# SyncE fetches one column of node rows in every second round of a four-layer graph network

## What is computed

```
x = layernorm(x + L0(x, src, dst))       # q,k,v: softmax over the edges of a node of q[src].k[dst]; sums v[src]
x = layernorm(x + L1(x, edge_attr_64))   # (x[src] + bond) @ W, softmax over the edges, sum, batch norm
x = layernorm(x + L2(x, edge_attr_64, _n2, _n3))  # message and key from [x[src], eh], query from [qrh, qeh]
x = layernorm(x + L3(x, edge_attr_32))   # relu([x[src], ea] @ w1 + b1) @ w2, mean over the edges, update
```

## Time and profile before

| | us |
|---|---|
| median of 3 runs | 9012.55 |
| the profiled execution | 9008.73 |
| its span, first to last instruction | 9006.9 |
| POOL busy | 6622.4 |
| DVE busy | 4898.5 |
| ACT busy | 3185.7 |
| PE busy | 2211.0 |

### The profile page before, as it was taken

The page is one execution under the profiler, slowest core; times in us unless marked ns, Lnnn a source line. Parts: engine busy times, 40 slices in busy tenths (PEclk is TensorE's granted clock), DMA queues, the critical chain, the costliest instruction groups (busy, mean ns, idle before and its releaser), DMA issues. The chain is left out here.

```text
span 9006.9 us, 54907 instructions
## 1 busy us (share of the span) xinstructions
PE 2211.0 (25%) x11915; PEld 1737.2 (19%) x11915; DVE 4898.5 (54%) x6124; ACT 3185.7 (35%) x3856; POOL 6622.4 (74%) x6997
## 2 busy tenths in 40 slices
PE   3000000000200000000046666666654222222224
PEld 1000000000200000000026666666643010101013
DVE  5356565655747777777744454444545333333335
ACT  0123222222513222232324555455544333333332
POOL 6777777777677777777757777777765777777776
PEclk6555555555555555555558888888877565656556
DMA  9233333333123333333323343434322333333332
GB/s 359 81 111 105 110 109 109 109 110 113 35 78 102 114 102 114 102 109 106 100 84 121 130 137 129 138 125 138 130 86 76 124 114 122 116 122 116 116 122 83
DMA packets 367104, 1037.46 MB, mean 115 GB/s; under 512 B 164320, under 2 KB 172410, under 8 KB 352272
## 3 DMA queue, kind: packets, MB, share of 16 engines
q1 hardware_dynamic: 136048, 670.35, 19.8%
q0 software_dynamic: 224608, 342.26, 14.7%
q10 hardware_dynamic: 6336, 23.79, 0.7%
HBM read 634.02 MB, written 401.90 MB: 115 GB/s over the span
## 5 line engine op out<-in xcount | busy, mean ns | idle before, releaser
L787 POOL DMA_INDIRECT g<-x_table,edge_ix x1512 | 1427.8, 944 | 460.8 <-issue 460.8
L787 POOL DMA_INDIRECT se<-x_table,edge_ix x1512 | 1426.8, 944 | 460.8 <-issue 460.8
L787 POOL DMA_INDIRECT hidden<-hidden_table,edge_ix x1512 | 1426.6, 944 | 460.8 <-issue 460.8
L787 POOL DMA_INDIRECT qv<-qv_table,edge_ix x1484 | 1400.2, 944 | 452.3 <-issue 452.3
L925 ACT ACTIVATE edge_sums<-edge_val 128x1904 f32<-128x1904 f32 (+3 forms) x220 | 1115.2, 5069 | 459.8 <-DVEq L1616 459.8
L915 DVE TENSOR_TENSOR_SCAN edge_val<-edge_bank,edge_val 128x464 f32<-128x464 f32 (+1 forms) x715 | 687.6, 1032 | 360.4 <-ACT edge_val L1578 354.0
L1570 PE MATMUL edge_e_ps<-w_nodes,edge_ea_t 128*128 128x512 f32 x784 | 474.8, 771 | 1466.9 <-DVEq L1610 1458.4
L868 ACT ACTIVATE edge_bank<-edge_weight_arg 128x112 f32<-128x112 f32 (+3 forms) x169 | 38.6, 228 | 2131.2 <-DVE edge_decay_arg L859 2131.2
L1609 DVE TENSOR_TENSOR hidden<-hidden,edge_e_ps 128x3584 f32<-128x3584 f32 x55 | 213.8, 3888 | 842.3 <-DMA hidden<-hidden_table,edge_ix 791.8
L1476 DVE TENSOR_TENSOR edge_product<-mk_ps,edge_q_now 128x256 f32<-128x256 f32 x392 | 166.6, 425 | 898.5 <-ACT edge_msg L1415 897.5
L1578 ACT ACTIVATE edge_val<-hidden 128x3584 f32<-128x3584 f32 x55 | 348.8, 6342 | 785.6 <-DVEq L1610 785.6
(11 more groups left out here) (425 smaller groups left out, 8468.6 us busy)
## 6 DMA issues: line engine op xcount, KB each, us to landing
sums<-edge_sums SPq DMA_DIRECT2D x56, 1848.0 KB, 7.0
sums<-edge_sums SPq DMA_DIRECT2D x55, 1792.0 KB, 6.2
sums<-edge_sums SPq DMA_DIRECT2D x56, 1008.0 KB, 4.0
sums<-edge_sums SPq DMA_DIRECT2D x55, 924.0 KB, 3.8
edge_k<-k_edges SPq DMA_DIRECT2D x56, 896.0 KB, 4.6
edge_bond<-in_edge_attr SPq DMA_DIRECT2D x56, 896.0 KB, 8.3
edge_eh<-in_edge_attr SPq DMA_DIRECT2D x56, 896.0 KB
edge_qr<-in_edge_attr_n SPq DMA_DIRECT2D x56, 896.0 KB
```

The costliest lines, as they stand in the source:

```text
L787: e.indirect_dma_start(self.gather_into(u, j), None, self.gather_from, bass.IndirectOffsetOnAxis(ap=now[:, j:j + 1], axis=0))\
```

## The change

In rounds 4, 6, ... 26 of layer 0, and 2, 4, ... 26 of the other layers, POOL leaves out the last column (27) of the chunk b = 1. SP fetches these 128 rows itself. It reads the 128 node numbers of the column, at most 22 at a time, from a new input `src_aside` in memory into registers, and issues for each number one transfer of one row, its address from the register, into one partition of a new tile `aside`. It does this in three portions (43, 43, 42 rows) in its turns for three chunks: both of the round before, and the first of the round itself. Behind the third portion it waits for all 128 rows and issues one transfer that copies `aside` into column 27 of the gather buffer (`place`). Then the hardware loop of SP has two rounds in its body. The last column of chunks b = 1 gets semaphores of its own, `last_in` when POOL gathers it and `placed` when SP does, and whoever waits for the last part waits for these as well.

```diff
@@ -32,6 +32,8 @@
 QUAD = 4
 ENDS, LATE = (4, 3), 3
 FD = 64
+BATCH = 22
+ASIDE = (slice(0, 43), slice(43, 86), slice(86, P))
 HEADS = 8
 FAR = -1.0e30
 SKIPPED = 1.0e9
@@ -79,6 +81,8 @@
         assert self.chunks % 2 == 0 and self.groups % 2 == 0 and J % QUAD == 0
 
         self.find_rows, self.find_cols = ins["dst_table"].shape
+
+        self.gather_width = (2 * FD, FD, FD, P)
 
         def dram(name, shape, dt=F32):
             return nc.dram_tensor(name, shape, dt).ap()
@@ -684,6 +688,10 @@
         self.part_summed, self.tail_ready = self.sem("part_summed"), self.sem("tail_ready")
         self.cut = 0
         self.passed = self.sem("passed")
+        self.steady = self.alone + 1
+        self.aside = self.sb("aside", [P, p.gather_width[layer]])
+        self.aside_in, self.placed = self.sem("aside_in"), self.sem("placed")
+        self.last_in = self.sem("last_in")
         self.bank = self.ps("bank", [P, 512])
         self.taken_of_bank = 0
         if h:
@@ -731,20 +739,54 @@
             e.sem_inc(self.stored[b], 1)
             load(b, b)
 
-        def turn(i):
+        def turn(i, beside=lambda b: None):
             for b in (0, 1):
                 for c in range(self.parts):
-                    self.wait_part(e, i, b, c)
+                    self.wait_part(e, i, b, c, placed=False)
                 load_index(b, bass.ds(i * (2 * J) + (2 + b) * J, J))
                 hold(e, self.attr_free[b], at(i, 1, 1), self.passed)
                 load(b, i * 2 + (2 + b))
+                beside(b)
                 hold(e, self.ready[b], at(i, 1, 1), self.passed)
                 store(b, rows_of(i, b, J))
 
-        for i in range(self.alone):
+        def fetch(k, rows):
+
+            for first in range(rows.start, rows.stop, BATCH):
+                now = slice(first, min(first + BATCH, rows.stop))
+                _, numbers = p.nc.values_load_multi_w_load_instructions(
+                    p.ins["src_aside"][bass.ds(k + (self.steady + 1) // 2, 1), now],
+                    engines=[mybir.EngineType.SP], min_val=0, max_val=p.n_rows - 1,
+                    skip_runtime_bounds_check_because="src holds node numbers below n_nodes")
+                for r, number in zip(range(now.start, now.stop), numbers):
+                    e.dma_start(self.aside[r:r + 1, :], self.gather_from[bass.ds(number, 1), :])\
+                        .then_inc(self.aside_in, 16)
+
+        def place(i, k):
+
+            hold(e, self.aside_in, at(k, 16 * P, 16 * P), self.passed)
+            hold(e, self.rows_free[1], at(i, 1, 1), self.passed)
+            u = self.buffer(i, 1)[0]
+            e.dma_start(self.gather_into(u, J - 1), self.aside[:, :]).then_inc(self.placed, 16)
+
+        e.sem_inc(self.placed, 1)
+        for i in range(self.steady):
             turn(i)
-        with e.Fori(self.alone, self.rounds - 1) as i:
-            turn(i)
+        with e.Fori(0, (self.rounds - 1 - self.steady) // 2) as k:
+            one = k * 2 + self.steady
+
+            def beside_one(b):
+                if b == 0:
+                    hold(e, self.placed, at(k, 16, 1), self.passed)
+                fetch(k, ASIDE[b])
+
+            def beside_two(b):
+                if b == 0:
+                    fetch(k, ASIDE[2])
+                    place(one + 1, k)
+
+            turn(one, beside_one)
+            turn(one + 1, beside_two)
         for b in (0, 1):
             if b and self.cut:
                 self.store_cut(e)
@@ -782,11 +824,27 @@
                     else:
                         e.wait_ge(self.rows_free[b], i + 1)
                 for j in range(J):
-                    if J * n + j < done:
+                    if J * n + j < done or (b and j == J - 1 and i in self.with_aside):
                         continue
                     e.indirect_dma_start(self.gather_into(u, j), None, self.gather_from,
                                          bass.IndirectOffsetOnAxis(ap=now[:, j:j + 1], axis=0))\
-                        .then_inc(self.gathered[u][j * self.parts // J], 16)
+                        .then_inc(self.last_in if b and j == J - 1 else self.gathered[u][j * self.parts // J], 16)
+
+    @property
+    def with_aside(self):
+        return range(self.steady + 1, self.rounds - 1, 2)
+
+    def wait_last(self, e, i, placed):
+
+        if isinstance(i, int) and i <= self.steady:
+            e.wait_ge(self.last_in, 16 * (i + 1))
+            return
+        alone = ((i + (2 + self.steady)) >> 1) * 16
+        if not placed:
+            hold(e, self.last_in, alone, self.passed)
+        else:
+            e.wait_ge(self.last_in, alone)
+            e.wait_ge(self.placed, at((i - (self.steady - 1)) >> 1, 16, 1))
 
     def buffer(self, i, b):
 
@@ -796,10 +854,25 @@
             return ((0, (0, 0, 1)), (1, (0, 0, 1)), (2, (0, 0, 1)), (0, (0, 0, 2)))[2 * i + b]
         return 1 - b, (i, 1, b)
 
-    def wait_part(self, e, i, b, c):
+    def wait_part(self, e, i, b, c, placed=True):
         u, (times, per, more) = self.buffer(i, b)
         columns = 16 * J // self.parts
-        e.wait_ge(self.gathered[u][c], at(times, per * columns, more * columns))
+        if c < self.parts - 1:
+            e.wait_ge(self.gathered[u][c], at(times, per * columns, more * columns))
+            return
+        if not self.begun:
+            e.wait_ge(self.gathered[u][c], at(i, columns - 16 * b, columns - 16 * b))
+        elif isinstance(i, int) and i < 2:
+            e.wait_ge(self.gathered[u][c], (columns, columns - 16, columns, 2 * columns - 16)[2 * i + b])
+        else:
+            more = columns if b else -16
+            if placed:
+                e.wait_ge(self.gathered[u][c], at(i, columns - 16 * b, more))
+            else:
+                hold(e, self.gathered[u][c - 1], at(i, columns, columns * b), self.passed)
+                hold(e, self.gathered[u][c], at(i, columns - 16 * b, more), self.passed)
+        if b:
+            self.wait_last(e, i, placed)
 
     def wait_gathered(self, e, i, b):
         for c in range(self.parts):
@@ -2552,6 +2625,8 @@
             full = a.reshape(1) if a.ndim == 0 else a
         arrays[name] = full
     arrays["src"] = arrays["src"].view(np.uint32)
+    ends = arrays["src"].reshape(P, edges_pp // (2 * J), 2 * J)[:, 0::2, 2 * J - 1]
+    arrays["src_aside"] = np.ascontiguousarray(ends.transpose(1, 0))
     return arrays
 
 
```

## The result

The changed kernel takes 9808.67 us (median of four runs, 9807.54 to 9812.9) where the kernel before takes 9011.03. The ratio is 1.0886, with a 95% interval of 1.0867 to 1.0905. The forecast was 8949.

What follows compares the result with a forecast made beforehand. POOL's unbroken row of gathers was taken as the bound: 51 fewer at 1.2485 us give 63.7 us, with SP's fetch and the waits free, so 9012.55 became 8949 us; own range 8943 to 8956, stated range 8940 to 8995.

Steps and rivals of the forecast that it cites:

- The forecast gain of 63.7 us: Edge phases on POOL: 51 gathers fewer, each taking away its whole pace of 1.2485 us.
- The cost on the path is nothing: SP's 128 row transfers and register loads per two rounds fit beside POOL's work and add no time.
- one trip a read: SP's reads of node numbers: six memory trips of 1.4 us per 128 rows, 0.07 us a row, plus 0.06 a number.
- c: Price on SP of one fetched row, number read included: taken as 0.62 us, with ends at 0.48 and 2.2.
- Late columns are free until POOL itself finds the buffer occupied: Placed column in layer 1: up to 15.8 us of lateness costs nothing, as VectorE frees the buffer before POOL returns.
- at about 0.9 us a row: Row price on SP where the change was to turn from gain into loss; lateness passes 15.8 us at 0.87.
- that formula: Lateness of the placed column in a pair of rounds, 128c - 95.7 us, once a row costs over 0.77 us.
- only the store and the next index list: What stands on SP behind the wait for all 128 rows; POOL wants the list a chunk later, so cost nothing.
- Rival A: SP's number reads: one memory trip per number, 1.96 us a row, SP becomes the bound, 15,300 us; chance 0.12.
- B: SP's small transfers disturb POOL's own issue in the fetching chunks: 89 us more than now, 9102 us; chance 0.04.
- C: Layer 1's saturated stretch delays SP's first rows, or row price near 0.88: part of gain lost, 8960 to 8995; chance 0.04.
- D: SP's row price sits on the crossing and the gain is just gone: 8995 to 9030 us; chance 0.03.

Runs made afterwards that it cites:

- the other order alone: Changed kernel, reads still unaligned, with SP's sums stored one turn later and its row fetch put ahead of the attribute-tile wait and load: 8984.4 us, ratio 0.9969.

## Why the prediction was wrong

**Right: what bounds the kernel and what a gather is worth.** The forecast gain of 63.7 us is what the kernel with aligned reads and an early fetch has: 9011.66 - 8947.81 = 63.9. The tail of the phases kept its length in that kernel, though not in the changed one. "The cost on the path is nothing" holds for the transfers alone: without the reads, 128 rows a pair are hidden in every layer.

**Mis-sized: the number.** I took 0.13 us a row ("one trip a read") for the read. Measured in layer 1 of the changed kernel: 587.6 us of reads and 104.8 of pointers in 13 pairs, so 53 us a pair or 0.42 us a row. The row's other terms, 0.50 by my sum, are 0.41 from start to start. So c was 0.83, not 0.62. The Trainium skill's 200 ns a register ("Runtime: NRT & Kernel Launch", section "Instruction fetch mechanics") lay between the two sorts: about 0.13 us a number at a boundary, 0.4 to 0.5 off it; the estimate of 0.76 a row from it was nearer than mine.

**The step that failed: "Late columns are free until POOL itself finds the buffer occupied", and with it "at about 0.9 us a row".** At 0.83 us a row that formula has lateness at 10.5 us, under the 15.8 that are free, and no loss. Measured: 19 us a pair. (In layer 2 c was 0.89, with 17.4 us of pointers a pair, and the formula with layer 1's slack has 2 us beyond the free ones; measured are 23.) And with the price as dear, the other order alone has no loss (8984.4 us). The formula let SP start the next pair on time whatever had happened in this one. But the fourth turn ends with the store of the sums, and those need the placed column first. In the pair printed above SP waits from 3178.84 to 3212.2 for them. I had named what stands behind the placing transfer on SP ("only the store and the next index list") and took it for harmless, and took 13.5 us for all that SP does beside rows. From the trace that part is the fourth turn, 36 us, the loop's end, 5.7, the three turns' index and attribute issues with their register work, 7.5, and the placement, 2: together some 52, and 159 - 106 = 53 us by the period. So the room was (138.6 - 53) / 128 = 0.67 us a row, not 0.87. With aligned reads a row is 0.63 us in layer 0 and 0.65 in layer 1, just inside, and that run shows it: layers 0, 1 and 3 at POOL's pace. With all reads moved off the boundary a row is 0.94 us in layer 1, which gives 53 + 120 = 173 us a pair, and 173 us lie between two placing transfers there.

**Not seen: layer 2's own chain**, by the attribute tiles. I had taken its slack from the timeline of the kernel before, where TensorE was on time. How much of its 5 us a pair with aligned reads is this chain and how much the dear pointers stays open.

**Not counted: the end of the loop.** Between the branch at the loop's end and SP's next instruction lie 4.5 to 5.7 us in every pair inside a phase (3052.32 to 3057.89 in layer 1). In the kernel before, with 32 to 40 recorded instructions in the body, most such gaps are 0.12 us; now the body has 482 to 498. The instruction queue moved 379 packets of 8 KB instead of 95. That fits a body that is fetched anew each time, but no run varied its length.

**The rivals.** Rival A had the side and the mechanism's place right (the reads of numbers, SP as the bound), with a price of 1.46 us a number where 0.42 was measured, and a crossing at 0.9 us a row where the room was 0.67. B, C and D are out. The chance of 0.81 for faster rested on an operation without a row, weighed at 12%, and on a room that I had worked out from a schedule without feedback.

## What to carry to other kernels

When work is added to a queue that also waits for other engines, don't compare its issue time with its idle time. Write down the closed chain: which wait stands behind the new work in program order, and does what it waits for depend on the new work? If so, the whole latency of that way counts in every round, and moving the wait one turn back, or the work ahead of it, can be worth as much as making the work cheaper: here order alone (both moves) was worth 824 us, alignment alone 800, and either took the whole loss away. For the whole gain of 64 us it took the aligned reads and the early fetch. An operation that no row of the trace shows deserves a wide price and a large chance.

## What the runs showed of the hardware

- A read of registers from memory depends on where it begins: 20 to 22 numbers take 2.1 to 3.9 us at a 16-byte boundary (up to 6.1 behind attribute loads) and 8.0 to 12.0 off it, with the same count.
- Each such read is preceded by one for the pointer, 1.1 to 1.5 us in a run's median and up to 6.4. The longest ones come directly behind attribute loads or, where the fetch stands ahead of these, 1.2 to 1.6 us behind the store of a chunk's sums.
- A transfer of one row with its address from a register is issued in 225 ns, one every 0.41 us; 128 of them beside 111 gathers leave the gathers at 944 to 945 ns.
- The end of a hardware loop on SP took 0.12 us with 32 to 40 recorded instructions in its body and 4.5 to 5.7 us with 482 to 498.
- A chip isn't like another: on one the kernel before took 11,421 us, 27% more, and 43 row transfers of SP took 52.4 us where they take 18.3 elsewhere, with POOL's gathers in layer 2 at 944 ns on both.
